# Early weight codes loaded from SyncE's queue, head scaling on VectorE, three-slot products on GpSimd, and re-ordered call lists in a decoder layer

## The reference

```python
x = x + attn(layernorm(x), Wq, Wk, Wv, Wo)      # 16 heads of 16, scores * tril, then softmax over all 128 keys
x = x + xattn(ctx, ctx, layernorm(x), ssm_kernel, D, 8)
#   kv[b,i,j,h,l] = k[b,h,i,l] * v[b,h,j,l]; y = causal convolution of kv with ssm_kernel[h] along l
#   out[b,j,h,l] = sum_i (y + kv * D[h])[b,i,j,h,l] * q[b,h,i,l]
x = x + ffn(layernorm(x), nvfp4 gate, up, down)  # codes looked up in a table, times a scale per block of 32
#   inter = gelu_tanh(xt @ Wg.T) * (xt @ Wu.T);  out = inter @ Wd.T;  MLP width 2048
```

## Time and profile before

| | before |
|---|---|
| median of three runs | 275.23 us |
| profiled execution, its own time | 275.35 us |
| its span, first to last instruction | 273.6 us |
| mean granted TensorE clock | 0.965 |
| busy: TensorE, VectorE, ScalarE, GpSimd | 249.4, 168.6, 129.9, 150.2 us |
| idle of TensorE over the span | 24.2 us |

### The profile page before, as it was taken

The page is one execution under the profiler, slowest core; times in us unless marked ns, Lnnn a source line. Parts: engine busy times, 40 slices in busy tenths (PEclk is TensorE's granted clock), DMA queues, the critical chain, the costliest instruction groups (busy, mean ns, idle before and its releaser), DMA issues.

```text
span 273.6 us, 5039 instructions
## 1 busy us (share of the span) xinstructions
PE 249.4 (91%) x1872; PEld 161.4 (59%) x1872; DVE 168.6 (62%) x264; ACT 129.9 (47%) x281; POOL 150.2 (55%) x188
## 2 busy tenths in 40 slices
PE   7999997599799699897799998999999999999993
PEld 7665764356566466676357575565566556655662
DVE  2889739954875959998898773441827355231225
ACT  2454654257565558865537563333325342532240
POOL 4278447716154966776957993337274455622330
PEclk9999999979979979999689999999999999999998
DMA  6998989710300304000000021000203000000004
GB/s 196 365 334 199 155 263 156 133 60 4 119 2 4 118 1 119 1 2 0 4 0 0 0 66 51 0 4 9 106 2 117 0 2 0 0 2 0 0 2 153
DMA packets 15104, 18.81 MB, mean 69 GB/s; under 512 B 1448, under 2 KB 12776, under 8 KB 15080
## 3 DMA queue, kind: packets, MB, share of 16 engines
q1 hardware_dynamic: 13832, 16.13, 22.3%
q10 hardware_dynamic: 1248, 2.36, 2.7%
HBM read 15.21 MB, written 3.15 MB: 67 GB/s over the span
## 4 chain that ended last, share of the span: by engine, by line
PE 54%; POOL 14%; DVE 11%; DMA 5%; issue 5%; ACT 4%; SPq 3%; ACTq 2%; DVEq 0%; POOLq 0%
PE bank L1257 27%; PE bank L1423 13%; POOL arena L437 5%; DMA XN<-in_down_scale 4%; PE bank L1329 3%; DVE arena L1028 2%; POOL QK L458 2%; POOL shift L342 2%; POOL rstd L340 2%; DVE mx L972 2%; PE bank L1313 2%; SPq L292 2%; PE bank L1311 2%; DMA X<-in_x 2%; PE bank L1315 1%
## 5 line engine op out<-in xcount | busy, mean ns | idle before, releaser
L458 POOL TENSOR_TENSOR QK<-QK 128x512 f16<-128x512 f32 x31 | 36.9, 1190 | 61.3 <-ACT QK L645 61.3
L1046 DVE SCALAR_TENSOR_TENSOR QK<-bank,QK 128x512 f32<-128x512 f32 x32 | 22.1, 690 | 63.5 <-PE bank L1257 63.3
L655 ACT ACTIVATE QK<-bank 128x512 f32<-128x512 f32 x32 | 19.1, 596 | 63.8 <-PE bank L1257 63.7
L1257 PE MATMUL bank<-xTh,Wa 128*128 128x512 f16 x128 | 42.6, 395 | 0.0
L1257 PE MATMUL bank<-xTh,Wb 128*128 128x512 f16 x128 | 40.7, 379 | 0.0
L437 POOL TENSOR_TENSOR arena<-Ys,qx 128x640 f32<-128x640 f32 x16 | 28.0, 1777 | 4.2 <-ACT qx L708 4.2
L1257 PE MATMUL bank<-xTl,Wa 128*128 128x512 f16 x64 | 25.3, 395 | 0.0
L1257 PE MATMUL bank<-xTl,Wb 128*128 128x512 f16 x64 | 24.3, 379 | 0.0
L1423 PE MATMUL bank<-Wb,QK 128*128 128x256 f16 x192 | 23.3, 273 | 0.9 <-POOL QK L458 0.9
L596 ACT ACTIVATE Ys<-bank 128x320 f32<-128x320 f32 x32 | 14.5, 453 | 19.6 <-PE bank L1315 12.3
L1423 PE MATMUL bank<-Wa,QK 128*128 128x256 f16 x192 | 23.6, 273 | 0.0
(11 more groups left out here) (145 smaller groups left out, 502.6 us busy)
## 6 DMA issues: line engine op xcount, KB each, us to landing
arena<-in_ker SPq DMA_DIRECT2D x2, 1024.0 KB, 12.6
QK<-qk_scratch SPq DMA_DIRECT2D x8, 256.0 KB, 5.9
arena<-in_ctx SPq DMA_DIRECT2D x2, 768.0 KB, 8.4
qk_scratch<-Wa SPq DMA_DIRECT2D x12, 128.0 KB, 3.2
arena<-in_codes SPq DMA_DIRECT2D x4, 384.0 KB
QK<-qk_scratch SPq DMA_DIRECT2D x8, 128.0 KB, 6.0
arena<-in_gu_scale SPq DMA_DIRECT2D x4, 256.0 KB
out<-XN SPq DMA_DIRECT2D x4, 256.0 KB, 2.4
```

Source lines behind the costliest of these rows:

```text
L458: g_.tensor_tensor(il[:, u % IR], val[:, u % VR], ih[:, u % IR], ALU.subtract).then_inc(s_il, 1)
L655: s_.activation(val[:, u % VR], bank[2 * (u % 2)][:, :], ACT.Gelu_apprx_tanh, scale=1.0 / W_GAIN).then_inc(s_gel, 1)
L1046: v_.scalar_tensor_tensor(out=val[:, u % VR], in0=bank[2 * (u % 2) + 1][:, :], scalar=UP_SCALE, in1=val[:, u % VR], op0=ALU.mult, op1=ALU. ...
L1257: ins = mmul(out, a(c), w(c), start=(n == 0), stop=(n == 3 * len(chunks) - 1))
```

## The change

- `load_codes(1)`, `(2)` and `(3)` are issued by SyncE, in its list of `max_rows` calls, and no longer by ScalarE.
- `scale_heads` is gone from GpSimd. `normalise(b)` on VectorE has it as a fourth instruction. `num` and `rec` have one buffer, s_o goes, and s_och counts four for each sequence.
- `near_products` is gone from VectorE. `conv_products(b, lc)` on GpSimd issues the three-slot product behind the five-slot one; s_z3 goes, s_z counts both. The low halves (`act_lo`) stay on GpSimd.
- CONV_EARLY is 8 instead of 13: heads 8 to 15 use bank 6 + lc.
- The call lists of TensorE, VectorE, ScalarE and GpSimd up to unit 8 are written in another order. The list from unit 8 on is the same.

```diff
-        num = sb("num", [P, 2, H, DH + 1])
-        rec = sb("rec", [P, 2, H])
+        num = sb("num", [P, H, DH + 1])
+        rec = sb("rec", [P, H])
...
-        CONV_EARLY = 13
+        CONV_EARLY = 8
...
-            for b in range(B):
-                max_rows(b)
+            def early_codes(j):
+
+                load_codes(sp, j)
+
+            max_rows(0)
+            early_codes(1)
+            max_rows(1)
+            max_rows(2)
+            early_codes(2)
+            max_rows(3)
+            early_codes(3)
+            max_rows(4)
...
-            def scale_heads(b):
-
-                pool.wait_ge(s_och, 3 * b + 3)
-                if b >= 2:
-                    pool.wait_ge(s_ot, b - 1)
-                g_.tensor_tensor(o_sb[:, b % 2, :].rearrange("p (h d) -> p h d", h=H), num[:, b % 2, :, 0:DH],
-                                 view(rec[:, b % 2], [[1, H], [0, DH]]), ALU.mult).then_inc(s_o, 1)
-
             def conv_products(b, lc):
...
+                g_.tensor_tensor(view(Z[:, r], [[64, H], [1, 3], [NSLOT, HD]], rows + NPAIR),
+                                 view(Ys[:, 0, 0], [every, [DIAG - 1, 3], [1, HD]], convolved + DIAG - 1),
+                                 view(qx[:, r], [[16, H], [-1, 3], [1, HD]], q + 3), ALU.mult).then_inc(s_z, 1)
...
             def decode_hi(j):
 
                 w_hi_step(j)
-                if j + 1 < EARLY:
-                    load_codes(sc, j + 1)
...
-                v_.reciprocal(rec[:, b % 2], num[:, b % 2, :, DH]).then_inc(s_och, 1)
+                v_.reciprocal(rec[:, :], num[:, :, DH]).then_inc(s_och, 1)
+                ve.wait_ge(s_och, 4 * b + 3)
+                v_.tensor_tensor(o_sb[:, b % 2, :].rearrange("p (h d) -> p h d", h=H), num[:, :, 0:DH],
+                                 view(rec[:, :], [[1, H], [0, DH]]), ALU.mult).then_inc(s_och, 1)
```

The end of TensorE's list before unit 8, with the loop that follows it in both:

```diff
             gate_and_up(5)
-            gate_and_up(6)
             turn_ffn(7)
+            down(5)
...
-            gate_and_up(7)
             for u in range(2 * EARLY, UNITS):
                 gate_and_up(u)
                 down(u - 2)
```

More of the change, by code:

```diff
@@ L1071, in _ @@
             x_lo(2)
-            q_lo(0, 2)
+            skip_tap(0)
             x_lo(3)
-            q_lo(0, 3)
             products(0)
             products(1)
+            q_lo(0, 2)
+            q_lo(0, 3)
+            skip_tap(1)
+            q_lo(1, 0)
+            skip_tap(2)
             products(2)
-            products(3)
-            q_lo(1, 0)
-            skip_tap(0)
             q_lo(1, 1)
-            skip_tap(1)
             q_lo(1, 2)
-            skip_tap(2)
             skip_tap(3)
             q_lo(1, 3)
+            products(3)
             skip_tap(4)
+            products(4)
             skip_tap(5)
@@ L1103, in _ @@
[L1103 to L1117 removed]
+            pair_max(0, 1)
+            decode_codes(0)
+            products(11)
+            pair_max(1, 0)
@@ L1118, in _ @@
+            products(12)
+            pair_max(1, 1)
+            skip_tap(14)
+            products(13)
+            pair_max(2, 0)
+            pair_max(2, 1)
+            products(14)
+            w_lo(0)
+            products(15)
+            skip_tap(15)
             decode_codes(1)
-            pair_max(2, 1)
             pair_max(3, 0)
             pair_max(3, 1)
+            normalise(0)
             pair_max(4, 0)
             w_lo(1)
+            stats_cross(0)
             pair_max(4, 1)
-            normalise(0)
+            normalise(1)
@@ L1557, in _ @@
             attend(0, 3)
+            convolve(15, 1)
+            key_scores(1, 1)
+            row_scores(3, 1)
             turn_max(2)
-            row_scores(4, 1)
+            attend(1, 0)
             turn_values(0)
+            row_scores(4, 0)
+            attend(1, 1)
+            attend(1, 2)
             turn_max(3)
-            row_scores(5, 0)
-            key_scores(1, 1)
-            attend(1, 0)
-            attend(1, 1)
-            turn_max(4)
-            key_scores(2, 0)
-            row_scores(5, 1)
@@ L1579, in _ @@
             attend(2, 2)
             attend(2, 3)
-            turn_max(5)
+            turn_query(0)
             key_scores(3, 1)
-            turn_heads(1)
-            row_scores(6, 1)
-            turn_query(0)
+            attend(3, 0)
             project_out(1)
-            attend(3, 0)
-            row_scores(7, 0)
+            turn_values(2)
             attend(3, 1)
-            turn_values(2)
-            key_scores(4, 0)
-            row_scores(7, 1)
+            turn_max(4)
+            row_scores(5, 1)
@@ L1593, in _ @@
             attend(3, 2)
             attend(3, 3)
+            turn_heads(2)
+            project_out(2)
+            row_scores(6, 0)
+            key_scores(4, 0)
+            turn_values(3)
+            key_scores(4, 1)
+            row_scores(6, 1)
+            attend(4, 0)
+            turn_max(5)
+            attend(4, 1)
+            attend(4, 2)
+            attend(4, 3)
+            row_scores(7, 0)
+            turn_query(1)
+            turn_heads(3)
+            add_cross(0)
+            key_scores(5, 0)
@@ L1609, in _ @@
[L1609 to L1611 removed]
             attend(5, 0)
+            attend(5, 1)
+            attend(5, 2)
             add_cross(1)
[L1614 removed]
+            turn_ffn(0)
+            attend(5, 3)
             key_scores(6, 0)
[L1616 to L1622 removed]
             turn_values(5)
@@ L1646, in _ @@
             turn_ffn(3)
-            turn_query(5)
-            turn_heads(7)
+            add_cross(4)
             gate_and_up(0)
-            project_out(7)
             gate_and_up(1)
-            add_cross(4)
+            turn_query(7)
             gate_and_up(2)
-            turn_query(6)
+            gate_and_up(3)
+            add_cross(5)
+            gate_and_up(4)
             down(0)
-            add_cross(5)
+            gate_and_up(5)
+            turn_ffn(4)
+            add_cross(6)
```

461 lines of the change are left out of this document (196 added, 265 removed).

## The result

The changed kernel takes **261.72 us** (median of 4 runs, 261.14 to 262.68) against 275.36 us (4 runs, 274.07 to 277.12) for the kernel before on the same chip: ratio 0.9504, 95% interval 0.9441 to 0.9567. The prediction was 261 us, range 254 to 270. The profiled execution took 262.25 us with a span of 260.5 us, 13.1 us less than before.

What follows compares the result with a forecast made beforehand. TensorE, 91% busy, loses time only to waits and slow clock, with GpSimd's chain mostly pacing the middle. Unit 8 begins 14.5 us earlier: 275.35 - 14.5 = 260.9, forecast 261 us, range 254 to 270.

Steps and rivals of the forecast that it cites:

- Convolutions, 6 us earlier: Convolutions: two TensorE waits (2.0 and 3.2 us) and 1.5 us of clock go, less 0.8; last convolution 6 us earlier.
- 0.8 us for single banks: Convolutions: heads 8 to 15 have one bank per half; two heads were counted as waiting 0.4 us each.
- First cross products at 79.0: Start of the middle: GpSimd's first cross products begin 11.6 us earlier, at 79.0 instead of 90.60 us.
- The prices: Moved operations: three-slot product on GpSimd 0.93 us (bounds 0.618 to 2.19), head scaling on VectorE 0.40 (0.38 to 0.99).
- the rival of 1.84 us: Three-slot product slow on GpSimd: at 1.84 us each the gain is gone, at 2.19 the time is 281; chance 0.09.
- GpSimd's chain to 156.3 us: Middle: GpSimd's 69.3 us of own work plus 8 of waits from 79.0 end act_lo(5) at 156.3 instead of 166.06.
- a middle in which the chain has left GpSimd: Sign against the forecast, which expected GpSimd busy above 85% from 80 to 155 us and in the chain.
- TensorE sets the pace: Rival: all TensorE waits and clock dips in the middle go but two us, 23 us less, 252 us; chance 0.13.
- Head scaling, 3.2 us of VectorE's time: Middle: eight scalings on VectorE cost 3.2 us there, while 16 three-slot products, 12.7 us, leave it.
- The queue rival: Rival: rows of maxima wait behind codes in SyncE's queue, key_scores(1, 0) 4 us late, 265 us; within main case's 0.52.
- Only the first part pays, 269 us: Rival: only the convolutions' 6 us are won, products and GpSimd's added 11 us take back the middle's gain; chance 0.20.
- Parts that add up: Whole kernel: each part of the change brings its own microseconds, summed to 14.5 us less at unit 8.

Runs made afterwards that it cites:

- experiment 6: The kernel before with only the DMA issues of codes 1 to 3 moved to SyncE, lists otherwise as before: 276.79 us, ratio 1.0041.
- experiment 5: The changed kernel with ScalarE issuing codes 1 to 3 inside decode_hi again: 266.55 us, ratio 0.9697 to the kernel before.
- 10: The changed kernel's new call lists with all three moves undone (codes issue, head scaling, three-slot products): 280.64 us, ratio 1.0177 to the kernel before.
- experiment 8: The changed kernel with CONV_EARLY 13 in place of 8: 261.25 us, ratio 0.9511 to the kernel before.
- experiment 1: The changed kernel without the three-slot products, part of the cross block left out: 261.94 us, ratio 0.9511 to the kernel before.
- experiment 4: The changed kernel with head scaling back on GpSimd and num and rec double-buffered again: 269.69 us, ratio 0.9776 to the kernel before.
- experiment 2: The changed kernel with each three-slot product issued twice on GpSimd, the first waited for: 275.43 us, ratio 1.001 to the kernel before.
- 2 x 2 table: Median times: old lists, moves undone 275.4 us, moves made 275.7; new lists, moves undone 280.6, moves made 261.7.
- experiment 11: The changed kernel with cross block 4 ahead of query 6 on TensorE and ScalarE: 263.98 us, ratio 0.9567 to the kernel before.
- experiment 12: The changed kernel with cross block 4 ahead of query 6, and codes 3 decoded later on VectorE: 261.62 us, ratio 0.9492 to the kernel before.

## Why the prediction held, step by step

The time was right to 0.7 us, the start of unit 8 to 1.4 us, and several steps were right as put. But two of its reasons were not, and that the number held all the same is in part luck: GpSimd's low half ends at 157.7 us and TensorE's own list reaches unit 8 at 159.73, so a sum over the wrong engine came out within 2 us.

**Convolutions, 6 us earlier.** Measured 5.0 us. The gaps of 2.03 and 3.22 us went, as put. The attribution was wrong: I gave 3.2 us to the codes on SyncE and 2.0 us to the later decoding. The first move alone gains nothing (experiment 6), and undone it leaves nearly all of the 5 us in place (last convolution at 64.28 and 64.59 us in experiments 5 and 10). Under the new lists ScalarE's stall doesn't come back even with its issues: at 52.47 us the three took 2.2 us, where in the kernel before the first alone kept ScalarE 3.56 us after its conversion. The 0.8 us for single banks don't show (experiment 8).

**First cross products at 79.0.** They began at 77.96 us.

**The prices.** Three-slot product on GpSimd 0.93 us predicted, 1.010 measured; head scaling on VectorE 0.40 and 0.424. Both were on the right end of their bounds, and the rival of 1.84 us fell with them.

**GpSimd's chain to 156.3 us: the step that failed.** Its end was right (the low half is done at 157.7), its role was not. My sum of 69.3 us own work and 8 us of waits described an engine that keeps up; GpSimd was busy 68.84 of 75 us between 80 and 155 us, as put. But taking 16 us away from it moves nothing (experiment 1). My own sign of failure, "a middle in which the chain has left GpSimd", came true: 3% of the chain. The reading behind it was too strong from the start: the chain of the kernel before goes through GpSimd for 35.7 of the 103 us from 70 to 173 us, and through TensorE for 30.6, which is not "most of the time"; only from 130 to 166 us is it 20.9 of 36. What sets the end now is TensorE's list, with 8.0 us of idle time from 62 us to unit 8, on VectorE and ScalarE for the most part, and none from 130 us on. That is the rival "TensorE sets the pace", whose mechanism holds and whose size was wrong: it let all waits but two us go, 252 us. With 8.0 in place of 2 us idle it would have come to 258, and to 260 with the 1.6 us of clock that the dip near 124 us costs at most.

**Head scaling, 3.2 us of VectorE's time.** Undone, the move costs 8.0 us: more than the 5 us of work that it puts on GpSimd, so the place in its queue counts (experiment 4). The Trainium skill (SBUF — State Buffer, "Who interferes with whom") speaks against a two-input VectorE operation beside GpSimd's products. The trace agrees and shows the price: of the eight scalings of 0.424 us one took 0.96 and one 1.66 us, the latter at 104.15 beside a product of GpSimd at 103.96. The other price, behind GpSimd's products, is higher.

**The queue rival.** No wait for the rows of maxima came in the changed kernel; TensorE waited for them where another queue had the codes (experiment 5). The rival's own case, rows behind codes, is there for sequences 1 and 3, with 7.4 and 5.6 us between issue and use, so how long they took stays unseen. The Trainium skill (DMA: Bandwidth & Descriptors, "Two DMAs through the same engine are not ordered") says that descriptors of one queue of one engine start in order. The trace agrees as far as it goes: the rows of sequence 2, issued from 66.48 us on ahead of codes 2, had landed when `key_scores` began at 69.30. The rule argues for the change only where rows are issued first.

**Only the first part pays, 269 us.** It did not happen, but its fear was sound: with GpSimd 18 us fuller the kernel is at 275.4 us (experiment 2).

**Parts that add up.** My sum took each part for itself. The 2 x 2 table refutes this. That neither the moves nor the lists would bring anything without the other stood nowhere in the prediction. It also counted the slow clock as time to be won, and for the kernel before the repeated executions show no such gain.

Open: how much the list of each engine brings by itself was not tried, nor the later decoding of codes 3 without experiment 11's order, which could be the faster of the two.

## What to carry to other kernels

When two engines end at nearly the same time, a sum over either gives the right number, and only taking work away from one tells which of them bounds. Price a moved operation by what stands ahead of it in the new queue and who waits behind it, not by its own length: 0.62 us of scaling cost 2.6 us of TensorE. Before counting a slow clock as lost time, compare executions at different mean clocks: where another engine sets the pace the loss may not show. And judge a reordering and the moves it makes room for together; tried one at a time, each half of this change would have been thrown away.

## What the hardware showed unexpectedly

- A DMA of 4 KB took 4.23 us beside 768 KB whose issue from another queue had begun 0.5 us earlier, and TensorE waited 2.03 us for it (experiment 5). Issued ahead of them in the same queue it was not waited for.
- One-element operations of GpSimd took 1.05 and 0.99 us instead of 0.55 and 0.27 beside VectorE's integer operations on 768 elements. In turn such an integer operation took 1.61 us instead of 0.53 to 0.56 beside GpSimd's products (experiment 12).
- The issue of the same DMA, the first of codes 1, kept ScalarE 5.02 us in the kernel before and 0.39 us in experiment 5, five microseconds later. What made the difference was not tried. Timelines of ScalarE:

```profile
47.59 5.02 ACTq L238 DMA_DIRECT2D XN<-in_codes  x1
...
52.47 0.39 ACTq L237 DMA_DIRECT2D XN<-in_codes  x1
```
- TensorE's clock fell behind a wait of 1.55 us at 123.60 us in the changed kernel and not behind one of 1.56 us at 123.90 in experiment 8.
